# Splitting the q and k columns at 256 instead of 296, taking two tiles with the first patch chunks, and draining the shared experts last, in a fused ViT block on one core

## What is computed

```python
tokens = einsum('bnd,ed->bne', patchify(x), W) + b        # 768 -> 256
h = concat([cls, tokens]) + pos_embedding                 # (16, 37, 256)
n = layernorm(h)
q, k, v = n @ Wq, n @ Wk, n @ Wv                          # 8 query heads, 4 key/value heads, D = 128
q, k = rotary(q), rotary(k)                               # q*cos + rotate_half(q)*sin
h = h + softmax(q k^T / sqrt(D), causal, per image) v @ Wo
n = layernorm(h)
shared = sum over 2 shared experts of gelu(n @ up_s) @ down_s
p = softmax(n @ router_w.T); gate = p at its top 4 of 16, else 0
routed = sum over 16 experts of gate[:, r] * gelu(n @ up_r) @ down_r     # computed for all experts
out = h + shared + routed
```

## Time and profile before

| | |
|---|---|
| median of three timed runs | 157.64 us (157.21 to 158.39) |
| the profiled execution | 157.14 us, of which the traced span is 155.4 us |
| PE busy | 147.8 us, 95% |
| DVE busy | 117.6 us, 76% |
| ACT busy | 101.9 us, 66% |
| POOL busy | 61.6 us, 40% |
| read from HBM / written | 11.05 MB / 0.61 MB |

### The profile page before, as it was taken

How to read it: one execution, slowest core, us unless ns; L and a number is a source line. 1 busy time by engine, 2 the same in 40 slices (tenths; PEclk the granted TensorE clock), 3 DMA queues, 4 the chain that set the end, 5 groups by cost and what they waited for, 6 DMA issues and landing times.

```text
span 155.4 us, 3279 instructions
## 1 busy us (share of the span) xinstructions
PE 147.8 (95%) x1089; PEld 138.3 (89%) x1089; DVE 117.6 (76%) x370; ACT 101.9 (66%) x290; POOL 61.6 (40%) x50
## 2 busy tenths in 40 slices
PE   6999989999999999999979999999999999999990
PEld 1887688899989998998969999999999999999990
DVE  0036886997887599758675656799999995999993
ACT  0304989964999988999785295995462934755310
POOL 0004898347748773244129100270532452235000
PEclk9999999999999999999999999999999999999998
DMA  5999900000000049960000000000000000000004
GB/s 154 347 375 370 371 20 0 0 0 2 6 0 0 0 141 422 418 245 0 2 0 4 0 0 0 0 4 2 2 0 4 0 2 0 0 4 0 4 2 156
DMA packets 5747, 11.88 MB, mean 76 GB/s; under 512 B 914, under 2 KB 3682, under 8 KB 5602
## 3 DMA queue, kind: packets, MB, share of 16 engines
q1 hardware_dynamic: 4434, 9.91, 17.2%
q10 hardware_dynamic: 1296, 1.75, 3.2%
HBM read 11.05 MB, written 0.61 MB: 75 GB/s over the span
## 4 chain that ended last, share of the span: by engine, by line
PE 75%; DVE 8%; DMA 5%; ACT 5%; SPq 3%; issue 2%; POOL 0%; DVEq 0%; POOLq 0%
PE bank L1027 62%; DMA wqkv_sb<-w_qkv 5%; DVE h L817 4%; PE bank L1144 4%; PE bank L1116 4%; PE bank L1132 2%; PE bank L1051 2%; ACT probs L487 2%; PE bank L1168 1%; PE bank L1071 1%; SPq L241 1%; SPq L238 1%; SPq L338 1%; ACT wqkv_hi L433 1%; ACT probsT L496 1%
## 5 line engine op out<-in xcount | busy, mean ns | idle before, releaser
L394 POOL TENSOR_TENSOR exp_lo<-ffn_sb,exp_hi 128x512 fp32r<-128x512 f32 x18 | 23.3, 1301 | 42.1 <-ACT exp_hi L509 42.0
L817 DVE SCALAR_TENSOR_TENSOR h<-bank,gate,h 128x256 f32<-128x256 f32 (+1 forms) x80 | 32.5, 473 | 1.5 <-PE bank L1027 1.3
L1027 PE MATMUL bank<-exp_lo,act_hi 128*128 128x256 f32 (+1 forms) x90 | 25.3, 281 | 0.0
L1027 PE MATMUL bank<-exp_hi,act_lo 128*128 128x256 f32 (+1 forms) x90 | 25.2, 280 | 0.0
L1027 PE MATMUL bank<-exp_hi,act_hi 128*128 128x256 f32 (+1 forms) x90 | 25.2, 280 | 0.0
L797 DVE TENSOR_TENSOR act_lo<-act,act_hi 128x256 fp32r<-128x256 f32 (+1 forms) x36 | 18.9, 548 | 4.9 <-ACT act_hi L521 4.5
L378 POOL TENSOR_TENSOR swapped<-swapped,sin_sb 128x592 f32<-128x592 f32 x12 | 17.8, 1485 | 11.3 <-ACT swapped L476 11.3
L1027 PE MATMUL bank<-hnT_hi,exp_hi 128*128 128x256 f32 (+1 forms) x72 | 21.8, 303 | 0.0
L1027 PE MATMUL bank<-hnT_hi,exp_lo 128*128 128x256 f32 (+1 forms) x72 | 21.5, 299 | 0.0
L1027 PE MATMUL bank<-hnT_lo,exp_hi 128*128 128x256 f32 (+1 forms) x72 | 21.5, 298 | 0.0
L518 ACT ACTIVATE act<-bank 128x256 f32<-128x256 f32 (+1 forms) x36 | 15.1, 419 | 9.2 <-PE bank L1027 9.0
(11 more groups left out here) (92 smaller groups left out, 371.1 us busy)
## 6 DMA issues: line engine op xcount, KB each, us to landing
ffn_sb<-w_ffn SPq DMA_DIRECT2D x6, 768.0 KB, 9.1
wqkv_sb<-w_qkv SPq DMA_DIRECT2D x4, 512.0 KB, 8.5
wo_sb<-w_o SPq DMA_DIRECT2D x1, 1024.0 KB, 11.0
x_sb<-xT ACTq DMA_DIRECT2D x3, 192.0 KB, 5.0
x_sb<-xT SPq DMA_DIRECT2D x3, 192.0 KB, 5.0
out<-h SPq DMA_DIRECT2D x2, 256.0 KB, 2.1
wp_sb<-wpT SPq DMA_DIRECT2D x3, 128.0 KB, 4.1
wp_sb<-wpT ACTq DMA_DIRECT2D x3, 128.0 KB, 5.3
```

Source lines behind the costliest of these rows:

```text
L394: nc.gpsimd.tensor_tensor(exp_lo[:, e % SPLIT_RING, :], ffn_sb[:, e, :], exp_hi[:, e % SPLIT_RING, :].bitcast(F32), ALU.subtract).then_inc ...
L817: last = nc.vector.scalar_tensor_tensor(h[r, i, :], y, gate[r, i, one], h[r, i, :], ALU.mult, ALU.add)
L1027: last = nc.tensor.matmul(ps, a, b, start=(n == 0 and m == 0), stop=(n == len(pairs) - 1 and m == 2 and not more))
```

## The change

The parts of the columns of q and k are now those of the experts, columns 0 to 255 and 256 to 591, in place of two halves of 296. A part no longer begins at an image's start, so the tables of cosines and sines have 370 columns and are read from an offset (`angles`). Groups of images become 3, 3, 3, 3, 2, 2; two of them lie wholly in the first part, and group 2 crosses into the second. `EARLY` goes from 3 to 2: the chunked patches hold two tiles, and three tiles have a DMA of their own. The experts are renumbered, the 16 routed ones 0 to 15 and the shared ones 16 and 17, which are summed in the last pieces, `down(17, p)`. Group, bank and wait numbers follow, `low_parts(0)` and `(1)` move ahead of the last three `normalise` steps on POOL, `high_parts(0)` and `(1)` forward on ACT, and the written-out orders of all engines are changed.

```diff
-HALVES = 2
-HT = IMAGES // HALVES * TOKENS
 T = IMAGES * TOKENS
-GROUPS = (3, 3, 2)
-NG = HALVES * len(GROUPS)
-GN = [g * TOKENS for g in GROUPS] * HALVES
+GROUPS = (3, 3, 3, 3, 2, 2)
+NG = len(GROUPS)
+GN = [g * TOKENS for g in GROUPS]
...
-EARLY = 3
+EARLY = 2
...
 SPANS = ((0, 2 * P), (2 * P, T))
 SPAN = max(z - a for a, z in SPANS)
+NS = len(SPANS)
+TURNS = max(a % TOKENS + z - a for a, z in SPANS)
...
-            return bank[(0, 1, 6, 5, 0)[i]]
+            return bank[(0, 1, 5, 4, 0)[i]]
...
-            return buf[:, first:second + 1:second - first, half(b)]
+            return buf[:, first:second + 1:second - first, span(b)]
...
+        def angles(b):
+
+            a, z = SPANS[b]
+            return slice(a % TOKENS, a % TOKENS + z - a)
...
-            return NP * max(0, e - NSHARED + 1) + p
+            return NP * min(e, NROUTED) + p
...
             normalise(0, 0)
+            sine(9)
+            sine(10)
             normalise(0, 1)
+            sine(11)
             normalise(1, 0)
             normalise(1, 1)
-            for n in range(9, 12):
-                sine(n)
             normalise(2, 0)
             normalise(2, 1)
             normalise(3, 0)
             normalise(3, 1)
             normalise(4, 0)
+            low_parts(0)
+            low_parts(1)
             normalise(4, 1)
             normalise(5, 0)
             normalise(5, 1)
-            for n in range(0, 18):
+            for n in range(2, 18):
                 low_parts(n)
...
-                if d == NP:
+                if d == 0:
...
             router_less_max()
+            act_low(4)
             act_low(5)
-            act_low(6)
+            top_gates()
+            add_expert(0, 0)
+            add_expert(0, 1)
+            add_expert(0, 2)
             add_expert(1, 0)
             add_expert(1, 1)
+            act_low(6)
+            act_low(7)
             add_expert(1, 2)
-            top_gates()
             add_expert(2, 0)
             add_expert(2, 1)
             add_expert(2, 2)
...
-                    pe.wait_ge(lo_made, tiles_with((b + 1) * HT))
+                    pe.wait_ge(lo_made, tiles_with(SPANS[b][1]))
                 if n >= 2:
                     pe.wait_ge(qk_cos, n - 1)
-                else:
-                    pe.wait_ge(h_kept, 3 + n)
+                elif n == 1:
+                    pe.wait_ge(h_kept, 4)
                 for j, head in enumerate(heads):
...
-                pe.wait_ge(qk_roped, PAIRS * (g // len(GROUPS)) + (c + 1) * PAIRS // 2)
+                pe.wait_ge(qk_roped, PAIRS * span_of(g) + (c + 1) * PAIRS // 2)
...
-                both = range(NSHARED) if e < NSHARED else (e,)
+                both = range(NROUTED, NEXP) if e >= NROUTED else (e,)
...
             for n in range(0, 6):
                 tokens_early(n)
-            for n in range(0, 3):
-                tokens_added(n)
+            tokens_added(0)
+            tokens_added(1)
+            tokens(2)
+            tokens_added(2)
             tokens(3)
             tokens_added(3)
             turn_norm(0)
+            turn_norm(1)
             tokens(4)
-            turn_norm(1)
+            tokens_added(4)
             turn_norm(2)
-            tokens_added(4)
             project(0)
             project(1)
             turn_norm(3)
             turn_norm(4)
-            values(0)
             project(2)
             project(3)
+            values(0)
             values(1)
-            values(2)
             project(4)
             project(5)
-            values(3)
+            scores(0, 0)
+            values(2)
             project(6)
             project(7)
-            scores(0, 0)
             scores(0, 1)
+            scores(1, 0)
             project(8)
-            scores(1, 0)
+            project(9)
             scores(1, 1)
-            values(4)
-            values(5)
-            project(9)
+            project(10)
+            project(11)
+            for n in range(3, 6):
+                values(n)
+            scores(2, 0)
             turn_probs(0, 0)
-            project(10)
             turn_probs(0, 1)
-            scores(2, 0)
             attend(0, 0)
             attend(0, 1)
-            project(11)
             scores(2, 1)
+            scores(3, 0)
             turn_probs(1, 0)
             turn_probs(1, 1)
-            scores(3, 0)
+            scores(3, 1)
             attend(1, 0)
             attend(1, 1)
-            scores(3, 1)
+            scores(4, 0)
+            scores(4, 1)
             turn_probs(2, 0)
-            scores(4, 0)
             turn_probs(2, 1)
-            scores(4, 1)
+            project_out(0)
             attend(2, 0)
             attend(2, 1)
-            project_out(0)
-            scores(5, 0)
             turn_probs(3, 0)
             turn_probs(3, 1)
-            project_out(1)
-            turn_norm(5)
+            scores(5, 0)
+            scores(5, 1)
             attend(3, 0)
             attend(3, 1)
+            turn_norm(5)
+            project_out(1)
+            project_out(2)
             turn_probs(4, 0)
             turn_probs(4, 1)
-            scores(5, 1)
+            turn_norm(6)
             attend(4, 0)
-            project_out(2)
-            turn_norm(6)
+            attend(4, 1)
             turn_probs(5, 0)
             turn_probs(5, 1)
-            attend(4, 1)
+            turn_norm(7)
             attend(5, 0)
-            turn_norm(7)
             attend(5, 1)
             project_out(3)
             project_out(4)
-            route(0)
+            up(0)
             turn_norm(8)
-            for n in range(0, 4):
+            for n in range(1, 4):
                 up(n)
             turn_norm(9)
-            for n in range(1, 5):
+            for n in range(0, 3):
                 route(n)
             up(4)
             up(5)
+            route(3)
+            route(4)
+            down(0, 0)
+            up(6)
+            down(0, 1)
+            up(7)
+            down(0, 2)
             down(1, 0)
-            up(6)
             down(1, 1)
+            up(8)
             down(1, 2)
-            up(7)
             down(2, 0)
...
             down(13, 2)
             down(14, 0)
-            up(32)
             down(14, 1)
+            for n in range(32, 36):
+                up(n)
             down(14, 2)
-            up(33)
-            up(34)
             down(15, 0)
             down(15, 1)
-            up(35)
             down(15, 2)
-            down(16, 0)
-            down(16, 1)
-            down(16, 2)
             down(17, 0)
             down(17, 1)
             down(17, 2)
...
-    ups = np.concatenate([np.asarray(L0_ffn_shared_up), np.asarray(L0_ffn_routed_up)])
-    downs = np.concatenate([np.asarray(L0_ffn_shared_down), np.asarray(L0_ffn_routed_down)])
+    ups = np.concatenate([np.asarray(L0_ffn_routed_up), np.asarray(L0_ffn_shared_up)])
+    downs = np.concatenate([np.asarray(L0_ffn_routed_down), np.asarray(L0_ffn_shared_down)])
...
-    cos_t = np.tile(np.cos(emb), (1, IMAGES // HALVES))
-    sin_t = np.tile(np.sin(emb) * sign, (1, IMAGES // HALVES))
+    cos_t = np.tile(np.cos(emb), (1, IMAGES))[:, :TURNS]
+    sin_t = np.tile(np.sin(emb) * sign, (1, IMAGES))[:, :TURNS]
```

315 lines of the change are left out of this document (162 added, 153 removed).

## The result

The changed kernel takes 156.53 us (median of 11 runs, 156.23 to 157.05), the kernel before on the same chips 157.50 (11 runs, 157.14 to 158.39). The ratio is 0.992 (0.990 to 0.994): 0.97 us less. The profiled execution took 156.23 us, of which 154.4 is span; before it was 157.14 and 155.4.

What follows compares the result with a forecast made beforehand. PE, busy 95%, was taken to bound the kernel. Front -0.5, projections +0.1, attention +0.2, router +1.0 and tail -0.9 sum to -0.1 us on 157.64; 157.4 us was forecast, range 156.2 to 158.3, eight in ten 155.4 to 159.2.

Steps and rivals of the forecast that it cites:

- front: Start to project(0): lighter chunks and new order remove 1.1 us, a table wait adds 0.8; 0.5 gain taken.
- projections and attention: From project(0) to the experts: 0.1 us lost to late swaps or cosines, 0.2 lost in attention.
- router to PE's end: Expert stage: PE stands still 1.0 us before down(1, 1), waiting for the first gated addition.
- tail: Behind PE's last matmul: DVE ends about 0.5 us behind PE instead of 1.6; gain 0.9.
- PE's question at 9.2: Front: PE through 24 chunk products at about 9.2, then waits 0.8 us for the table's operands, ready at 10.1.
- the gain of 0.3 plus "up to 0.3": Front: removed 1.1, added 0.8 gives 0.3 us; lighter chunks may start PE up to 0.3 earlier.
- 0.5 instead of the 0.8 wait: Attention: turn_norm(6) and (7) have about 2.3 us of cover under a chain of 2.8, so PE waits 0.5.
- 0.3 by my layout: Attention: project_out(2) waits 0.3 us for keep_turned(5) and heads_low(3, 1).
- R: Router: the end of route(4), from which PE's arrival at down(1, 1), R + 4.3, and the additions' end, R + 5.3, are counted.
- the gate product meets POOL's low part: Second rival, at the router: DVE's gate product held by POOL's expert 4 low part, wait 2.3 for 1.0, 158.7 us; chance 0.16.
- the fourth: Rival: front's wait becomes the table wait, router's is covered, only the tail's 0.9 gained: 156.7 us; within forecast's range, 0.47.
- the first: Rival: router wait 0.5 or less, front gives 1.1, attention's wait goes, tail 0.9: 155.6 us; chance 0.25.

Runs made afterwards that it cites:

- the kernel with the low parts moved: Changed kernel with five slots, up(8) and up(9) moved ahead, and act_low(6) and act_low(7) each put ahead of an addition on DVE: 0.991, 156.06 us.
- the new front alone: Changed kernel's front and attention, with the experts, their numbers and orders of the kernel before: 0.988, 155.72 us; repeated on another chip 0.989.
- one shared expert first: Changed kernel with one shared expert drained first and the other last, each alone, 54 pieces added and not 51: 1.003, 158.16 us.
- The second trace with that front and order: Kernel before up to and with project_out(4), then the changed kernel's experts (shared experts last): 1.002, 158.06 us.
- no table: Changed kernel with the router's exponential replaced by a copy with 32 added, so no activation table loads there: 0.991, 156.43 us.
- five slots: Changed kernel with five weight slots instead of four and expert 4's parts made ahead of the router: 0.992, 156.14 us.
- the kernel with both causes out of the way: Changed kernel with five weight slots, expert 4's parts made before the router, and up(8), up(9) moved ahead of down(1, 1): 0.988, 155.73 us.

## Why the prediction was right or wrong

**The sign and the size.** I forecast a net of -0.1 us by the sum (157.54; 157.4 was said, leaning without a term for it) and it was -1.0, inside the range. Within 1%, the likeliest class, holds narrowly, but a measurement does tell it from none: the interval ends at 0.994. Each term against its stage:

| term | forecast | bounds | measured |
|---|---|---|---|
| front | -0.5 | +0.3 to -1.1 | -0.9 in the profiled pair, -0.7 to -1.0 by the medians |
| projections and attention | +0.3 | +2.4 to -0.8 | -0.5 |
| router to PE's end | +1.0 | +0.5 to +2.3 | +1.5 |
| tail | -0.9 | -0.4 to -1.2 | -1.0 |

That the time lies in the range is in part luck: the first two terms were 0.4 and 0.8 us too cautious and the third 0.5 too hopeful. The prediction had also named its own sign of failure, new waits for qk (cosine) or for probsT. Both came, 0.4 and 0.2 us, so its picture of the projections and the attention is refuted by its own test, though the price was small.

**Front: right in its steps, too small in size.** "The operands are ready at 10.1" was 10.08, and the first addition waits for them. I put PE's question at 9.2. It comes later, near 10: PE's 24 starts in the chunks lie 1.0 us further apart in all than its step of 0.22 there. Three other executions book 0.2 to 0.3 of such time to the DMA of the patches; the rest is booked to nothing. In the kernel with the low parts moved the chunk products ended at 9.83, and the wait for the table was 0.3. So the 0.8 us between PE's own rate and the table are partly chunks and partly table, but the end is the same. All ten executions with two tiles in the chunks that I looked at have the first `tokens_added` 1.58 to 1.59 after DVE starts on the table. Three of them, `aux_high` and `tokens_added`: 8.35 and 9.94 in the new front alone, 8.64 and 10.23 in the changed kernel, 9.50 and 11.08 with one shared expert first:

```profile
9.50 0.29 DVE L852 CAST aux_high<-aux_sb 64x256 fp32r<-64x256 f32 x1 [8.37 <-DMA aux_sb<-aux_w]
```

```profile
11.08 0.48 PE L1088 MATMUL bank<-aux_parts,aux_pick 128*128 128x256 f32 x2 [0.82 <-DVE aux_parts L857]
```

So `project(0)` lies between 19.17 and 20.09 in nine executions with the new front, the middle one 19.56. I had said 19.6, but as a gain of 0.5 on 20.16, and 20.16 belongs to the fastest of eleven executions of the kernel before. The second trace with that front and order, 19.91, is the fastest of its twelve as well. Fast against fast, the gain is 0.92. By the medians it is 0.7 to 1.0: 0.97 us of time, less what the other three stages gave and took, with 0.5 to 0.7 for the attention's. That 19.6 itself was met is luck: it was counted from a fast execution, and an ordinary one came out there. The term that was too small is the gain of 0.3 plus "up to 0.3"; which of its parts was short is not separated by any run.

**Projections and attention: wrong in sign.** I took 0.1 lost in the projections and 0.2 in the attention, and 0.5 was gained (0.5 to 0.7 in nine executions with this attention). The two steps that failed: "0.5 instead of the 0.8 wait" for `turn_norm(6)` and `(7)`, and "0.3 by my layout" for `project_out(2)`. Neither wait exists. `turn_norm(7)` of the changed kernel:

```profile
78.86 0.44 PE L1097 MATMUL bank<-ident,hn 128*128 128x128 f32 x2
```

Two transposes and two calls of `attend` were cover enough. With the 0.2 for heads_lo, 1.0 of waits went; 0.41 for `cosine(0)` and 0.2 for `keep_pT` came. Their difference, 0.4, is near the stage's 0.46. Of these two, the second is the one that I named ("`attend(0, 0)` follows straight on `turn_probs`: 0.15 to 0.3 lost"):

```profile
54.01 1.77 PE L1170 MATMUL bank<-probsT,v_sb 111*128 111x222 f32 x8 [0.24 <-ACT probsT L516]
```

The first I had at the wrong pair. I looked for a late swap among the pairs of 672 columns at the end, where ACT is fullest, and none came late. It is at `project(2)`, behind pairs of 256 columns at the start:

```profile
23.23 0.39 PE L1053 MATMUL bank<-hnT_hi,wqkv_hi 128*128 128x256 f32 x1 [0.41 <-DVE qk L733]
```

There the pair is short (1.4 us of PE) and ACT and DVE still have norms of the last tiles in front of the swap. The narrow part makes PE's cover shorter, and that I had priced for the wide one only. These steps are read from the traces; no run puts one of them back alone.

**Router: place and size right, what follows it wrong.** R was 93.3. PE came to `down(1, 1)` at 97.58, R + 4.3, and went on at 98.58, R + 5.3, both as forecast. Inside, two small errors cancel: ACT ended the exponential at R + 1.95 and not 2.25, and from there to PE's start it was 3.3 us and not 3.0, for hand-overs that I had left out (0.14 between the second addition's end and PE's start) and for a second addition that counts with its whole 0.48.

The price was right, and the experiments show the reason incomplete. I treated the gates as the one chain. Three things are due within a microsecond: the gates, the low part of expert 4 and DVE's backlog. With the gates 0.6 earlier (no table) the stage is as long as before. With the second alone (five slots) the stop stays and the stage is 0.4 shorter, by the small gaps behind. With both out of the way it is 0.8 shorter, and the third is left. My sentence "after that the pieces wait no more by my layout" failed: summed over PE's starts from the experts on, what lies over the usual step is 0.3 us before and 1.7 after, 1.1 of it at the stop and 0.4 in small ones between 113.9 and 116.3. Busy time by stretch (PE, PEld, DVE, ACT, POOL):

```profile
98.58:116.50 17.92, 17.92 (x141) 17.64 (x142) 16.97 (x39) 10.28 (x27) 7.77 (x6) 1.00 0.01 2
116.50:140.00 23.50, 23.50 (x188) 23.49 (x187) 21.05 (x51) 13.28 (x35) 9.19 (x7) 1.00 0.01 2
```

DVE is busy 95% for 18 us behind the gates and 90% after. I had compared one addition with one piece (0.8 against 0.7) and seen a cover; over a row of pieces that comparison says the opposite, that DVE doesn't gain on PE. The second stop of the kernel with both causes out of the way bears this out, 3 us behind the gates. The gaps from 113.9 on are another matter. DVE had come level before them: it stood idle for 0.92 us, until ACT's next high part, and then its low part met POOL's:

```profile
111.40 2.21 DVE L822 TENSOR_TENSOR act_lo<-act,act_hi 128x256 fp32r<-128x256 f32 x3 [0.92 <-ACT act_hi L541]
111.29 1.29 POOL L411 TENSOR_TENSOR exp_lo<-ffn_sb,exp_hi 128x512 fp32r<-128x512 f32 x1 [1.61 <-ACT exp_hi L529]
```

The first of the three low parts took 1.46 us, where one of this size takes 0.42 without POOL. PE's gap there ends at 114.16, 0.15 after the first addition that stands behind the three. An earlier one, at 104.73, took 1.48 for 0.50. So 2.0 us of DVE's 95% are time in which POOL held it. In the kernel with five slots the stop at the gates is the same, the meetings fall otherwise (0.7 us before 114), and the small gaps are gone; no run changes the meetings alone.

**POOL was not met at the gates, but elsewhere.** I gave 0.16 to the case that the gate product meets POOL's low part. They missed each other by 0.5 us (97.41 and 97.92), and L811 took 0.24 where the like took 1.17 before. In no variant does the gate product meet it. What I overlooked is that the same meeting happens all through the expert stage, in every trace: four to six of DVE's 36 activation low parts (`act_low`, two SBUF tiles) take longer beside POOL's low parts, six with 3.2 us over their usual time in the kernel before and 4.1 in the changed one, up to 1.0 for one. The rule of the Trainium skill that I cited, SBUF — State Buffer, section Who interferes with whom, is in line with these and with the 0.24. I had priced it for one instruction only, and the new experts have 0.9 us more of it.

**The tail: right.** "About 0.5 behind PE" was 0.45. It gave 1.0 for 0.9.

**The rival that came nearest** in time is the fourth, 156.7, though not for its reason: it had the tail alone, with the router's wait covered. In mechanism the first, 155.6, is nearer: its front and its attention came for the most part, and its hidden router wait did not.

## What to carry to other kernels

When a wait goes away at the end of a kernel by changing the order of work, look for what the old order had been covering at the other end: here the shared experts' ungated additions were the cover of the router, and the move alone is a loss. Where PE stops for the last of several things that are due within a microsecond, removing that one buys only the distance to the next, so list what is due there before pricing a remedy. And compare a helper engine with PE over a whole stretch and not for one step, and look in its busy time for steps that take longer than their like: here 2.0 of 17 us were DVE held by POOL, not work.

The version with five slots and two units ahead of the first gated piece (0.988, 155.73 us) has the lowest ratio of the change's kind, and the new front with the old experts (0.988 and 0.989) is as good. Both intervals reach into that of the changed kernel on other chips (0.987 to 0.992), so a lead over it is not shown.

## What I had not expected of the hardware

DVE could start on the table between 8.35 and 9.50 in ten executions of kernels with the same first transfers, and most of this spread of 1.15 us goes into the start of `project(0)`: it lies 10.6 to 11.0 us behind the table in the nine with the new front. A front of this kind has to be judged over many runs, and a single execution held only against one of like rank: by the estimates above, the fastest of one kernel against an ordinary one of the other would have shown 0.6 or 1.3 us for 0.9. Also, a matmul's modelled end can hide a real wait of some tenths: the list of waits shows none for the table in the changed kernel's execution, while the constant 1.58 us across executions does.
